# Second attention: value tiles issued in pairs, the later pair ahead of the maxima's transposes

## The reference, cut to what matters

```python
fused = x @ w_qkv.T + b_qkv
q = fused[..., :256]; k = fused[..., 256:320]; v = fused[..., 320:]
q = q.reshape(B, S, 8, 4, 8).transpose(0, 2, 3, 1, 4)
k = k.reshape(B, S, 8, 8).transpose(0, 2, 1, 3)
v = v.reshape(B, S, 8, 8).transpose(0, 2, 1, 3)
sim = einsum('bgrsd,bgtd->bgrst', q, k) / sqrt(8)
out = einsum('bgrst,bgtd->bgrsd', softmax(sim), v)
```

## Time and profile before

| | |
|---|---|
| runs | 1117.79 us median of 3 (1117.62 to 1119.75) |
| the profiled execution | 1118.09 us, of which 1116.3 us are its span |
| TensorE matmul | 1004.6 us busy (90%), 5701 instructions |
| VectorE | 762.9 us (68%), 1575 instructions |
| ScalarE | 591.3 us (53%), 894 instructions |
| GpSimd | 315.5 us (28%) |
| granted TensorE clock, mean | 0.967 of full speed |
| the second attention | first maxima's transposes at 459.11 us, last value tile over at 902.17 us |

### The profile page before, as it was taken

The page is one execution under the profiler, slowest core; times in us unless marked ns, Lnnn a source line. Parts: engine busy times, 40 slices in busy tenths (PEclk is TensorE's granted clock), DMA queues, the critical chain, the costliest instruction groups (busy, mean ns, idle before and its releaser), DMA issues.

```text
span 1116.3 us, 17223 instructions
## 1 busy us (share of the span) xinstructions
PE 1004.6 (90%) x5701; PEld 735.6 (66%) x5701; DVE 762.9 (68%) x1575; ACT 591.3 (53%) x894; POOL 315.5 (28%) x330
## 2 busy tenths in 40 slices
PE   4999998789999575999999999999999987999996
PEld 3877876689999533555545555555555565888885
DVE  6577556566655257799898888888888756444438
ACT  6325553565555453466655665666566655444431
POOL 2004777256744400000000122222221000455432
PEclk9999998899999886999999999999999998999998
DMA  6863333655344352121111222222222124333244
GB/s 235 308 277 127 104 128 110 206 160 157 122 135 134 129 238 34 18 34 28 22 29 29 44 57 58 57 57 57 57 57 44 64 83 149 110 106 105 86 175 174
DMA packets 48962, 120.20 MB, mean 108 GB/s; under 512 B 7736, under 2 KB 24760, under 8 KB 48344
## 3 DMA queue, kind: packets, MB, share of 16 engines
q1 hardware_dynamic: 18960, 66.15, 20.3%
q0 software_dynamic: 11760, 32.24, 7.6%
q10 hardware_dynamic: 18160, 20.71, 6.5%
HBM read 72.17 MB, written 52.29 MB: 111 GB/s over the span
## 4 chain that ended last, share of the span: by engine, by line
PE 66%; DVE 14%; POOL 6%; ACT 5%; DMA 4%; issue 3%; SPq 0%; ACTq 0%; DVEq 0%; POOLq 0%
PE psum L815 11%; PE psum L837 10%; PE psum L824 8%; PE psum L630 5%; PE psum L631 4%; PE psum L632 4%; POOL xg L462 4%; DVE work_f L1721 4%; PE psum L544 3%; PE psum L545 3%; PE psum L546 3%; PE psum L616 2%; PE psum L641 2%; ACT work_f L1214 1%; DVE x L1321 1%
## 5 line engine op out<-in xcount | busy, mean ns | idle before, releaser
L1721 DVE TENSOR_REDUCE work_f<-psum 128x1 f32<-128x512 f32 x512 | 334.9, 685 | 51.1 <-PE psum L815 49.7
L1214 ACT ACTIVATE work_f<-psum 128x1024 f32<-128x1024 f32 x172 | 168.9, 1023 | 111.9 <-PE psum L824 110.3
L815 PE MATMUL psum<-work_r 128*128 128x512 f32 x512 | 205.3, 440 | 20.0 <-DVE work_f L1721 7.1
L469 POOL DMA_INDIRECT yk<-yb,dest x133 | 129.2, 971 | 238.7 <-ACT yb L1060 209.9
L815 PEld LDWEIGHTS psum<-work_r 128*128 128x128 f32 x512 | 94.2, 190 | 131.5 <-DVE work_f L1721 75.8
L824 PE MATMUL psum<-qm,work_r 128*128 128x512 f32 x512 | 161.8, 398 | 4.2 <-ACT work_f L1214 2.7
L462 POOL DMA_INDIRECT xg<-xn,slot x112 | 108.3, 967 | 180.5 <-PE psum L853 152.3
L824 PEld LDWEIGHTS psum<-qm,work_r 128*128 128x128 f32 x512 | 93.6, 188 | 31.8 <-ACT work_f L1214 10.9
L630 PE MATMUL psum<-wexp,xbh 128*128 x266 | 101.6, 382 | 9.3 <-issue 4.3
L1214 ACT ACTIVATE pt<-psum 128x1024 f32<-128x1024 f32 x84 | 82.8, 1023 | 50.2 <-PE psum L824 49.3
L631 PE MATMUL psum<-wexp,xbh 128*128 x266 | 95.7, 360 | 0.0
(11 more groups left out here) (218 smaller groups left out, 2035.3 us busy)
## 6 DMA issues: line engine op xcount, KB each, us to landing
xb<-xg ACTq DMA_DIRECT2D x62, 258.0 KB
xg<-in_pad SPq DMA_DIRECT2D x1, 10320.0 KB
yg<-yk SPq DMA_DIRECT2D x20, 512.0 KB, 9.3
stage<-in_moe SPq DMA_DIRECT2D x16, 608.0 KB, 5.2
xg<-in_pad SPq DMA_DIRECT2D x1, 7224.0 KB
work_r<-work_r SPq DMA_DIRECT2D x128, 48.0 KB
work_r<-work_r SPq DMA_DIRECT2D x32, 192.0 KB
stage<-in_moe SPq DMA_DIRECT2D x16, 384.0 KB, 3.8
```

Of the source, the lines that this page charges most:

```text
L469: nc.gpsimd.indirect_dma_start(yk[l], bass.IndirectOffsetOnAxis(ap=dest[:, j % 8, i:i + 1], axis=0), yb[l][:, j % 2, i, :], None).then_inc ...
L815: nc.tensor.matmul(next_bank(pe, ("scores", n), b_mx, n + 1), qs[g % 2][:, t * P:(t + 1) * P], km[g % 4][:, r, :], start=True, stop=True). ...
L1214: nc.scalar.activation(pt[((b * NG + g) * QT + t) % 3][:, 2 * h:2 * h + 2, :], psum[:, 3 + 2 * h:5 + 2 * h, :], ACT.Exp, scale=float(HD) * ...
L1721: v.reduce_max(mx[:, s % 2, i:i + 1], ring["scores", n], AX.X).then_inc(b_mx, 1)
```

## The change

The lists of steps are new; no instruction is added or taken away. On TensorE value tiles 0 and 1 stand together at step 12, tiles 2 and 3 together at step 2 of the next stage, behind score 2 and ahead of the maxima's transposes, which `stage` now issues behind the parts of unit s - 2. The steps of `scores_t` are 5, 6, 8, 10, 11, 13, 14 and 16 in place of 4, 5, 8, 11, 12, 13, 16 and 17. The outputs move from step 11 to 10, the values by key from 12 to 8, and the projection from 13 to 8; VectorE's `compact`, `normalise` and copy follow by the same numbers. ScalarE copies the outputs ahead of exponent 0 and does `compact` ahead of exponent 3.

```diff
         def turns(s, following):
             never = QT * R
-            return {"maxima": 2, "outputs": 11, "values": 12 if s == NG + 1 else never,
-                    "project": 13 if following and NG - 3 <= s < NG else never}
+            return {"maxima": 2, "outputs": 10, "values": 8 if s == NG + 1 else never,
+                    "project": 8 if following and NG - 3 <= s < NG else never}
...
-            TRANSPOSED = (4, 5, 8, 11, 12, 13, 16, 17)
-            VALUED = (15, 15, 19, 25)
+            TRANSPOSED = (5, 6, 8, 10, 11, 13, 14, 16)
+            VALUED = (12, 12, 18, 18)
...
                     if front:
                         scores(b, s, i)
-                    if i == turn["maxima"] and back:
-                        maxima_t(b, s - 1)
                     if i == TRANSPOSED[0] and back:
                         pe.wait_ge(b_qm, b * NG + s)
                     if s >= 2:
                         follow(b, s - 2, QT * R + i)
+                    if i == turn["maxima"] and back:
+                        maxima_t(b, s - 1)
                     if back:
                         follow(b, s - 1, i)
...
                         for h in range(2):
-                            if s >= 2 and s % 2 and (t, h) == (1, 1):
+                            if s >= 2 and s % 2 and (t, h) == (0, 0):
                                 outputs(b, s - 2)
+                            if (t, h) == (1, 1) and following and NG - 3 <= s < NG:
+                                compact((0, 2, 1)[s - (NG - 3)], b + 1, ring["projection", b * 3 + s - (NG - 3) + 4], s - (NG - 3))
                             act.wait_ge(b_st, b * (2 * NG * QT) + ((g * QT + t) * 2 + h + 1))
...
-                    if t == 2 and following and NG - 3 <= s < NG:
-                        compact((0, 2, 1)[s - (NG - 3)], b + 1, ring["projection", b * 3 + s - (NG - 3) + 4], s - (NG - 3))
```

## The result

1136.5 us median of 4 runs (1134.8 to 1137.94) against 1118.77 of the kernel before, measured beside it: ratio 1.0161, 95% interval 1.0146 to 1.0176. The profiled execution took 1136.65 us with a span of 1134.8, 18.5 us more than the span of before.

What follows compares the result with a forecast made beforehand. It took a nearly gapless TensorE as the bound, VectorE as near second. Terms 3.7 + 1.0 + 4.5 + 6.3 - 1.4 + 0.8 + 0.3 = +15.2 us on 1118.09 gave 1133.3, range 1125 to 1141.

Steps and rivals of the forecast that it cites:

- plain: Stretches without outputs, projection or values by key, walked step by step: 13.18 against 12.87 us, 12 times, +3.7 us.
- outputs: Stretches with outputs and no projection: normalise falls into the value pair; 13.69 against 13.53 us, six times, +1.0 us.
- projection: Stretches with a projection, no outputs: score 11 waits 2.00 us for the bank; 16.29 against 14.78, three times, +4.5 us.
- projection and outputs: Stretches with both: the outputs' transposes wait 1.48 us for the bank; 16.12 against 15.07, six times, +6.3 us.
- values by key: Stage 9, three times: values by key at step 8, no more wait for normalise; 14.4 against 14.90 us, -1.4 us.
- VectorE's small operations: Stages 3 to 5 of the first sequence: they delay five maxima behind qm by about 0.1 each; +0.8 us.
- first stretch, tail: First stretch gets a value pair ahead of the next M, +1.1; the tail has one less, about -0.8; together +0.3 us.
- M: Start of the maxima's transposes on TensorE, the zero point from which the walk counts times in a stretch.
- The pairing: Value tiles 2 and 3 together on TensorE save 0.15 us plus a slow restart and entry of 0.10 each: 0.35 a unit.
- rival 1: Only the pairing counts: each unit gains 0.35 us and nothing waits, 1107 us; chance 0.05.
- Rival 2: The maxima's wait is covered (qm ends within 0.93 of M), the projection's isn't: near 1117 us; chance 0.07.
- Rival 3: Value pairs are split because tile 3 waits 0.3 us more a unit for exponent 7: +9, 1142 us; chance 0.08.

Runs made afterwards that it cites:

- project11: The changed kernel with the projection at step 11 instead of 8 and ScalarE's compact ahead of exponent 4; 1123.88 us.
- pair_only: The kernel before with only tile 3 of the values moved from step 9 to step 3 of the next stage, beside tile 2; 1131.89 us.
- straddle: project11 with value tile 3 at step 3 instead of 2, so one tile stands on each side of the maxima's transposes; 1113.2 us, ratio 0.9948.
- maxfirst: The changed kernel with the maxima's transposes directly behind score 2, ahead of the value pair of step 2; 1149.54 us.
- spacing_only: The kernel before with only the steps of the transposed scores changed to 5, 6, 8, 10, 11, 13, 14, 16; 1133.93 us.
- compact_late: The changed kernel, projection still at step 8, with only ScalarE's compact moved behind exponent 3; one run of 1162.04 us.
- tile3_behind: The changed kernel, projection still at step 8, with only value tile 3 moved from step 2 to step 3 of the next stage; 1129.07 us.
- outputs13: The kernel before with the outputs' transposes at step 13 instead of 11 in the nine stages with outputs and no projection; 1115.99 us.
- both: The changed kernel with the projection at step 11 and the maxima's transposes ahead of the value pair; 1140.05 us.

## Why the prediction was right, and where it was off

The forecast was 1133.3 us, slower, in a range of 1125 to 1141. Of the 31 stretches and the tail, in us:

| | count | forecast, each new stretch | measured | forecast sum | measured sum |
|---|---|---|---|---|---|
| plain | 12 | 13.18 | 13.16 to 13.21, the first four 13.34 to 13.63 | +3.7 | +4.5 |
| outputs | 6 | 13.69 | 13.52 to 13.67, stage 3 of the first 14.35 | +1.0 | +1.7 |
| projection | 3 | 16.29 | 16.34 to 16.36 | +4.5 | +4.7 |
| projection and outputs | 6 | 16.12 | 16.28 to 16.31, first 16.76 | +6.3 | +7.9 |
| values by key | 3 | 14.4 | 14.54, 14.55, first 16.89 | -1.4 | -1.4 |
| VectorE's small operations | | | (in the rows above) | +0.8 | |
| first stretch, tail | | | 13.43, 12.33 | +0.3 | +0.5 |
| sum | | | | +15.2 | +17.9 |

- **The plain walk** held step by step: `qm` starts at 0.69 behind M (forecast 0.74), score 5 at 1.44 (1.57), score 12 at 5.94 (5.95), score 13 at 8.12 (8.13). Only the wait at score 5 was about 0.5 and not 0.64; what it lacks came back at VectorE's pace further on.
- **The projection** was the large term by forecast and by measurement: 12.6 of the 17.7 us go when it moves back under a pair (project11). The waits were 1.47 and 1.90 where the walk had 1.48 and 2.00. The term for stretches with outputs was mis-sized, 16.12 against 16.29: the bank came free where the walk had it (643.60 is 7.88 behind its M; the walk's distances add up to 7.85), but the score behind the outputs' transposes then cost 0.32 and not 0.23, and other small steps between it and the next M made up the rest. The first sequence adds VectorE's small operations.
- **Outputs:** `normalise` does fall into the pair; the wait of the earlier trace rows is gone.
- **Values by key:** that the sum agrees to 0.1 us is partly luck. The ordinary two take 14.55 and not 14.4, and the first, 16.89 after 17.55, gains more than the others.
- **The pairing** gives what the earlier trace rows say: the two tiles of a pair start 0.88 apart (628.78, 629.66), where a lone tile costs 1.00. The rule of the Trainium skill that a change of the tiling mode drains the engine ("TensorEngine Tiling (Array Packing)", Key Properties) agrees with the rows; that it alone would decide (rival 1, 1107) is refuted by pair_only, slower with fewer switches, and by straddle, faster than project11 with more.
- **Rival 2** (the wait of the maxima covered) fell at its own condition: `qm` ends 1.38 behind M (623.21 + 0.69) and not within 0.93, and VectorE stands still for 0.92 ahead of it. **Rival 3** (pairs split by exponents) did not come: the pair of tiles 2 and 3 takes 1.85 from its start to the transposes (633.87 to 635.72), with no wait for exponent 7 in it.
- What the prediction did not see, and the experiments did, is the second wait at the maxima, ahead of them. It was covered in both kernels, so no term of the sum depended on it, but my expectation for maxfirst did. That VectorE idles behind each pair was in the walk as a fact without a price; maxfirst and pair_only show it: there the pair is followed by a row of ten or twelve maxima at VectorE's pace.

Open: the spacing of the transposed scores was not varied with values at step 12, so whether straddle is the best order is not known. ScalarE's copy of the outputs ahead of exponent 0 was not taken back alone either; straddle keeps it and is faster than the kernel before.

## What to carry to other kernels

When work is moved off a spot to be grouped elsewhere, ask what it covered there: here lone value tiles hid the way from a transpose through VectorE and back, and a value pair hid the way from a projection through two engines, and together these cost more than the switches saved. The reader of a ring of three banks ran dry behind a long block: VectorE stood still for 0.80 to 1.31 us behind a pair of 1.85 in the rows shown, and for 0.37 behind a lone tile in straddle. Here the blocks were better spread, one on each side of a round trip. A walk through one turn of the loop with start-to-start distances from the trace gave stretch lengths within 0.2 us, provided that every bank and buffer wait is in it; the walks for maxfirst and spacing_only, which lacked one, were wrong by more than 10 us in the total.

## What was not expected of the hardware

TensorE's granted clock fell in some stretches in which the engine stood still longer, in an otherwise busy window. Waits of 3.15 and 3.58 us in compact_late were followed by it in six cases of nine, with a mean clock of 0.84 to 0.92 over the stretch, and the nine stretches grew by 27.4 us in all where the waits alone make 16.6. Shorter waits were followed by it too. A wait of 1.73 us in tile3_behind stands ahead of the window at 0.66, with a stretch 1.65 us longer. And at the start of the second sequence, where the maxima's transposes wait for VectorE, the stretch behind the wait has a mean clock of 0.88 after 1.74 us in straddle and in tile3_behind and after 1.91 us in outputs13, and of 0.82 after 2.73 us in maxfirst and in both; in maxfirst the 5 us from 600 are at 0.50 throughout. The row of straddle:

```profile
589.91 1.02 PE L853 MATMUL psum<-const,work_r 128*128 128x128 f32 x4 [1.74 <-DVE work_f L1721]
```

There the kernel before waits 1.07 us and the changed kernel 0.88 us, both at a clock of 1.00. The changed kernel's profiled execution shows 1.00 behind its waits of 1.30 and 1.73 us as well. A wait in TensorE can thus cost more than its length, and waits of the same length are not always followed by it; what decides it in a given case these runs don't show.
